# A two-layer block on one core: x loaded behind the weights, the prologue sorted by group, and the third group's projections moved into the recurrence

## What is computed

```python
q, k, v = silu(x @ Wq), silu(x @ Wk), silu(x @ Wv)          # x is layer-normed first
log_f = log_sigmoid(x @ Wf1 @ Wf2)
gamma = -sigmoid(x @ Wg)
k = l2norm(k);  a = k * gamma[..., None]                    # 16 heads of 8
def step(S, inp):                                           # over the 1024 tokens
    S1 = S + a[:, None] * (k @ S)[None]
    S2 = exp(gf)[:, None] * S1
    S3 = S2 + a[:, None] * (k @ S2)[None] + k[:, None] * v[None]
    return S3, q @ S3
out = layernorm(o * sigmoid(x @ Wo1 @ Wo2)) * ln_w @ Wout
x = x + out                                                 # only the last third of the o rows is used
x = x + shared_ffn(layernorm(x)) + top1_of_16_experts(layernorm(x))
```

## Time and profile before

| | us |
|---|---|
| median of 3 runs | 670.8 (670.62 to 671.29) |
| the profiled execution | 673.13 |
| its span, first to last instruction | 671.4 |
| busy in the span: PE, DVE, ACT, POOL | 528.3, 492.5, 248.9, 360.0 |
| mean granted TensorE clock, share of full | 0.917 |
| GpSimd / VectorE / TensorE share of the chain that ended last | 12%, 33%, 30% |

### The profile page before, as it was taken

One profiled execution on the slowest core, in us unless ns is written; L12 is line 12 of the kernel. 1 busy time (PEld: TensorE's weight loads), 2 busy tenths in 40 slices (PEclk: granted clock), 3 DMA queues, 4 the chain that ended last, 5 costly groups with the idle time before them and its releaser, 6 DMA issues.

```text
span 671.4 us, 7382 instructions
## 1 busy us (share of the span) xinstructions
PE 528.3 (79%) x1809; PEld 273.7 (41%) x1810; DVE 492.5 (73%) x809; ACT 248.9 (37%) x515; POOL 360.0 (54%) x349
## 2 busy tenths in 40 slices
PE   1768989999999886877387689879999967578930
PEld 1434434444454433322154455525454255345520
DVE  3369999989898998799589999498999775412201
ACT  1825754444445242111122145533545124135520
POOL 4235767666667575654567333366767574700023
PEclk9868999999999998887799799998999977979985
DMA  9601116700000590000611012300100021112224
GB/s 218 138 0 32 32 42 162 217 0 1 0 1 0 141 356 35 1 0 0 170 35 55 17 48 69 110 15 16 31 23 18 0 52 35 43 56 63 63 80 111
DMA packets 46706, 41.79 MB, mean 62 GB/s; under 512 B 4588, under 2 KB 40248, under 8 KB 46168
## 3 DMA queue, kind: packets, MB, share of 16 engines
q1 hardware_dynamic: 43140, 35.61, 18.9%
q0 software_dynamic: 2400, 5.38, 2.7%
q10 hardware_dynamic: 1136, 0.46, 0.3%
...
## 4 chain that ended last, share of the span: by engine, by line
DVE 33%; PE 30%; issue 16%; POOL 12%; DMA 5%; ACT 2%; ACTq 1%; POOLq 0%; DVEq 0%; SPq 0%
DVE grown L1412 9%; PE ps L1874 6%; DVE early L1527 5%; POOL grown L1062 4%; DVE ps L1451 4%; PE ps L1831 4%; PE ps L1891 3%; DVE early L1532 3%; PE ps L1832 2%; PE ps L1931 2%; DVE grown L1439 2%; POOL uv L978 2%; PE ps L1639 2%; DVE grown L1405 2%; POOL early L1009 2%
## 5 line engine op out<-in xcount | busy, mean ns | idle before, releaser
L1062 POOL TENSOR_TENSOR grown<-grown 128x512 f32<-128x512 f32 x64 | 80.8, 1272 | 101.4 <-DVE grown L1439 101.4
L1412 DVE TENSOR_TENSOR grown<-ps,steps 128x1536 f32<-128x1536 f32 x64 | 112.1, 1752 | 1.8
L1831 PE MATMUL ps<-grown,cst 128*128 128x512 f32 x128 | 77.7, 692 | 27.8 <-DVE grown L1412 27.6
L857 ACT ACTIVATE uv<-ps 128x512 f32<-128x512 f32 x64 | 38.1, 597 | 110.5 <-DVE grown L1439 110.5
L1874 PE MATMUL ps<-steps 128*128 x128 | 69.6, 642 | 8.8 <-issue 8.6
L1832 PE MATMUL ps<-grown,cst 128*128 128x512 f32 x128 | 71.4, 641 | 0.0
L978 POOL TENSOR_TENSOR uv<-uv,steps 128x512 f32<-128x512 f32 x64 | 67.7, 1081 | 1.7 <-ACT uv L857 1.6
L1310 DVE TENSOR_TENSOR e_h<-rk,ps 128x256 f32<-128x256 f32 x64 | 25.4, 417 | 53.8 <-ACT rk L870 34.0
L1839 PE MATMUL ps<-uv,cst 128*128 128x512 f32 x128 | 60.4, 594 | 0.4 <-POOL uv L978 0.4
L1117 POOL TENSOR_TENSOR early<-state,qT 128x512 f32 x22 | 37.2, 1690 | 32.4 <-DVE state L1426 32.4
L1088 POOL COPY early<-early 128x32 f32<-128x32 f32 x63 | 27.5, 436 | 43.9 <-DVE early L1532 43.9
...
...
## 6 DMA issues: line engine op xcount, KB each, us to landing
...
```

The lines of the kernel that those rows point to most:

```text
L1062: G.tensor_tensor(decayed[:, h], decayed[:, h], work[:, h, 1], ALU.add).then_inc(s_add[h], 1)
L1412: V.tensor_tensor(grown[:, :, h].rearrange("p e (x w) -> p e x w", w=HD), st, per_col(tile, FF, 3, h, HD), ALU.mult).then_inc(s_prod[h], 1)
L1831: T.matmul(bank[2 * h + 1], c["block"], work[:, h, 1], start=True, stop=True).then_inc(s_usum[h], 1)
```

## The change

- SP loads x in four parts: groups 0 and 1, group 2, then, only after the constants and all weights but Wq have landed, the other 12 tiles of the first 21, and the last 11. The weights have three semaphores: Wk and Wv, the five small ones, Wq.
- The batches of the layer norm are tiles 0 to 4, 5 to 20 and 21 to 31.
- ScalarE gets two one-column activations, which load the Sqrt table before the first variances are there, and the Silu table right behind the first root.
- TensorE begins with the transposes and K of group 0; `low` and `wfo` (the products of the small weights) come between. ScalarE, GpSimd and VectorE have group 0 ahead of group 1 likewise.
- The start copies of the state move ahead of the statistics of the third part of x and wait only for their own two banks; the other banks are waited for where TensorE first writes them. c_keys(0) moves behind the first pass, the statistics of the last 11 tiles behind the second, c_keys(1) into step 1's corrections, p_of(1) into the loop.
- K and V of group 2 move into step 0's `front`, G and F into step 1's.

```diff
+    if i == 0:
+        found += [("K", 2), ("V", 2)]
+    if i == 1:
+        found += [("G", 2), ("F", 2)]
...
-FIRST = [("low", 0, 7), ("wfo", 0, 7), ("xT", 0, 0), ("xT", 1, 1), ("K", 0, 2), ("K", 1, 3), ("V", 0, 4), ("V", 1, 5),
-         ("squares", 0, 6), ("squares", 1, 7), ("G", 0, 0), ("F", 0, 1), ("G", 1, 2), ("F", 1, 3), ("xT", 2, 4),
-         ("rk", 0, 5), ("rk", 1, 6), ("K", 2, 0), ("V", 2, 1), ("c", 0, 7), ("c", 1, 2), ("G", 2, 3), ("F", 2, 4)]
+FIRST = [("xT", 0, 0), ("K", 0, 2), ("low", 0, 7), ("xT", 1, 1), ("V", 0, 4), ("K", 1, 3), ("wfo", 0, 7), ("V", 1, 5),
+         ("squares", 0, 6), ("squares", 1, 7), ("G", 0, 4), ("F", 0, 5), ("G", 1, 1), ("F", 1, 3), ("rk", 0, 6),
+         ("rk", 1, 7), ("xT", 2, 4), ("c", 0, 6), ("c", 1, 5)]
...
+        warm = sb("warm", [P, 2])
...
-        s_cst, s_cst2, s_xf, s_wa = sem("s_const"), sem("s_const_rest"), sem("s_xf"), sem("s_attn_weights")
-        s_x = [sem(f"s_x_part{k}") for k in range(3)]
+        s_cst, s_cst2, s_xf, s_wa = sem("s_const"), sem("s_const_rest"), sem("s_xf"), sem("s_low_weights")
+        s_wkv, s_wq = sem("s_key_value_weights"), sem("s_query_weights")
+        s_x = [sem(f"s_x_part{k}") for k in range(4)]
...
-        LN_BATCH = [5, 25]
+        LN_BATCH = [5, 21]
...
-            split = GROUPS[1][0]
-
...
+            first, third = GROUPS[1][0], GROUPS[2][0]
...
-                sp.dma_start(xr1[b * C:(b + 1) * C, split:, :], x_tokens(b, split, L1)).then_inc(s_x[0], 16)
+                sp.dma_start(xr1[b * C:(b + 1) * C, first:, :], x_tokens(b, first, L1)).then_inc(s_x[0], 16)
...
-                sp.dma_start(xr1[b * C:(b + 1) * C, 0:split, :], x_tokens(b, 0, split)).then_inc(s_x[1], 16)
+                sp.dma_start(xr1[b * C:(b + 1) * C, third:first, :], x_tokens(b, third, first)).then_inc(s_x[1], 16)
+            sp.wait_ge(s_cst, 16)
+            sp.wait_ge(s_wa, 80)
+            sp.wait_ge(s_wkv, 32)
...
-                sp.dma_start(xr2[b * C:(b + 1) * C, :, :], x_tokens(b, L1, NT)).then_inc(s_x[2], 16)
+                sp.dma_start(xr1[b * C:(b + 1) * C, 0:third, :], x_tokens(b, 0, third)).then_inc(s_x[2], 16)
+            for b in range(B):
+                sp.dma_start(xr2[b * C:(b + 1) * C, :, :], x_tokens(b, L1, NT)).then_inc(s_x[3], 16)
...
-            for dst, src in ((wqkv[:, 1], "Wk"), (wlow[:, 0], "Wf1"), (wlow[:, 1], "Wo1"), (wup[:, 0], "Wf2"),
-                             (wup[:, 1], "Wo2"), (wgs[:], "Wg"), (wqkv[:, 2], "Wv"), (wqkv[:, 0], "Wq")):
+            act.dma_start(wqkv[:, 1], a["Wk"]).then_inc(s_wkv, 16)
+            for dst, src in ((wlow[:, 0], "Wf1"), (wlow[:, 1], "Wo1"), (wup[:, 0], "Wf2"), (wup[:, 1], "Wo2"),
+                             (wgs[:], "Wg")):
...
+            act.dma_start(wqkv[:, 2], a["Wv"]).then_inc(s_wkv, 16)
+            act.dma_start(wqkv[:, 0], a["Wq"]).then_inc(s_wq, 16)
...
+            S.activation(warm[:, 0:1], eps[:], ACT.Sqrt)
...
+            S.activation(warm[:, 1:2], eps[:], ACT.Silu)
+            evict("xT", 0, xnT[0][:, 0:wide_of(0)], cols=wide_of(0))
+            evict_slot("K", 0, K, ACT.Silu)
+            k_square(0)
...
+            evict("xT", 1, xnT[1][:, 0:wide_of(1)], cols=wide_of(1))
+            evict_slot("V", 0, VV, ACT.Silu)
+            evict_slot("K", 1, K, ACT.Silu)
+            k_square(1)
...
-            for n in (0, 1):
-                evict("xT", n, xnT[n % 2][:, 0:wide_of(n)], cols=wide_of(n))
-            for n in (0, 1):
-                evict_slot("K", n, K, ACT.Silu)
-                k_square(n)
-            for n in (0, 1):
-                evict_slot("V", n, VV, ACT.Silu)
+            evict_slot("V", 1, VV, ACT.Silu)
...
-            for n in (0, 1):
-                evict_slot("G", n, Y, ACT.Sigmoid)
-                evict_slot("F", n, FF, ACT.Sigmoid)
-                spread_rk(n)
+            evict_slot("G", 0, Y, ACT.Sigmoid)
+            spread_rk(0)
+            evict_slot("F", 0, FF, ACT.Sigmoid)
+            spread_rk(1)
+            evict_slot("G", 1, Y, ACT.Sigmoid)
+            evict_slot("F", 1, FF, ACT.Sigmoid)
...
-            evict_slot("K", 2, K, ACT.Silu)
-            k_square(2)
-            evict_slot("V", 2, VV, ACT.Silu)
-            evict_slot("G", 2, Y, ACT.Sigmoid)
-            evict_slot("F", 2, FF, ACT.Sigmoid)
...
-            pool.wait_ge(s_wa, 128)
+            pool.wait_ge(s_wa, 80)
...
-            for n in (0, 1):
-                gate_keys(n)
-                y_of(n)
-                y_keys(n)
-            for n in (0, 1):
-                p_of(n)
+            gate_keys(0)
+            y_of(0)
+            y_keys(0)
+            gate_keys(1)
+            y_of(1)
+            p_of(0)
+            y_keys(1)
...
-                if i in NEED[2:]:
+                if i in NEED[1:]:
...
+            def begin(h):
+
+                V.tensor_copy(bank[2 * h].rearrange("p (x w) -> p x w", w=HD),
+                              c["diag8"].unsqueeze(1).to_broadcast([P, P // 2, HD])).then_inc(s_state[h], 1)
+
...
-            ln_shift(0)
...
+            ln_shift(0)
...
+            ln_stats(LN_BATCH[0], ORDER.index(GROUPS[3][0]))
+            dve.wait_ge(s_cst, 16)
+            for h in (1, 0):
+                dve.wait_ge(s_taken[2 * h], PORT_FIRST[2 * h])
+                begin(h)
...
-            ln_stats(LN_BATCH[0], LN_BATCH[1])
+            ln_stats(ORDER.index(GROUPS[3][0]), LN_BATCH[1])
...
-            ln_shift(1)
...
+            ln_shift(1)
...
-            c_keys(0)
-            ln_stats(LN_BATCH[1], NT)
-            c_keys(1)
...
-            def begin(h):
-
-                V.tensor_copy(bank[2 * h].rearrange("p (x w) -> p x w", w=HD),
-                              c["diag8"].unsqueeze(1).to_broadcast([P, P // 2, HD])).then_inc(s_state[h], 1)
-
...
-            for b in range(6):
-                dve.wait_ge(s_taken[b], PORT_FIRST[b])
-            for h in (1, 0):
-                begin(h)
-                step(h, 0)
-            front(0)
+            step(1, 0)
+            c_keys(0)
+            step(0, 0)
+            dve.wait_ge(s_x[3], 16 * B)
+            ln_stats(LN_BATCH[1], NT)
...
+                if i == 1:
+                    c_keys(1)
...
+                if kind == "Q":
+                    pe.wait_ge(s_wq, 16)
...
-            pe.wait_ge(s_wa, 128)
+            x_transposes_of(0)
+            pe.wait_ge(s_wkv, 32)
+            project("K", 0)
+            pe.wait_ge(s_wa, 80)
...
+            x_transposes_of(1)
+            project("V", 0)
+            project("K", 1)
...
-            for n in (0, 1):
-                x_transposes_of(n)
-            for kind in ("K", "V"):
-                for n in (0, 1):
-                    project(kind, n)
+            project("V", 1)
...
+            rk_over_heads(0)
+            rk_over_heads(1)
...
-            for n in (0, 1):
-                rk_over_heads(n)
-            project("K", 2)
-            project("V", 2)
-            for n in (0, 1):
-                head_sum(n)
-            project("G", 2)
-            project("F", 2)
+            head_sum(0)
...
+                if i == 0:
+                    pe.wait_ge(s_taken[2 * h + 1], PORT_FIRST[2 * h + 1])
...
+                if i == 0:
+                    pe.wait_ge(s_taken[4 + h], PORT_FIRST[4 + h])
...
+                else:
+                    head_sum(1)
```

## The result

The changed kernel takes **666.89 us** (median of 5 runs, 666.41 to 667.84) where the kernel before takes 670.8 (669.66 to 671.29): a ratio of 0.9947, 95% interval [0.9932, 0.9961]. That is faster, but by 3.9 us and not by 9.4; 661.4 was forecast. The profiled execution took 666.89 with a span of 665.1, 6.3 less than the span before, whose own execution lay 2.3 above its median.

A forecast was written before the change was run, and what follows sets the result against it. Bound by a chain of waits before the loop, opening with the last attention weight's transfer, and a full settled loop: −15.8 at the first pass, +2.7, +1.2, +2.5 in steps 0 to 2, sum −9.4, 661.4 us; range 658 to 667.

The forecast's parts named there:

- Mark A: Start of the loop's first pass: forecast to move from 40.90 to 25.1 us, 15.8 earlier.
- The weights: Prologue: weights taken as landed by 7.5 us, with 0.58 MB of x and 0.42 MB of weights and constants asked for.
- Rival 2: Prologue: weights do not land earlier, their queue taking turns with x; first pass at 31, −3 us, 668; chance 0.12.
- q10's 12.2%: First 16 us: the weights' queue keeps 16 engines busy 1.95 us, so its own packets do not explain landing at 13.3.
- Pace of TensorE: Prologue: slow K, V and eight records of group 1 assumed; at 2.4 GHz, −1.5 and −1.0 us more.
- Step 0: Loop: head sum of group 1 comes last, +2.7 us; with TensorE at 2.4 GHz the statistics come last, step 10.3.
- Step 1: Loop: K, V and square sums of group 2 queue ahead of the step's sums on TensorE, +1.2 us.
- step 2: Loop: a new Sqrt table load delays the last root and VectorE's reciprocal, +2.5 us.
- B: Start of the same loop pass in step 3: forecast to move from 66.45 to 57.0 us.
- What is gained at B should stay: After step 3's pass: same rows in same order, reloads tied to loop steps, so the −9.4 us should last.
- rivals 3 and 4: Clock slower in steps 1 to 3, +11, 682 (0.03); gain taken back later, within 1 us of no change (0.04).
- Rival 1: Third group's work hides better in the loop, TensorE entering at 2.4 GHz: −12 to −13 us, 658; chance 0.13.

The follow-up runs named there:

- the experiment: Changed kernel with GpSimd's two buffer clearings made to wait until group 1 is normalized: 662.46 us, ratio 0.987 to the kernel before.
- x not held: Changed kernel with GpSimd's clearings behind group 1's normalization and SP's three waits ahead of the rest of x removed: 663.93 us, ratio 0.9892.
- three fixes: Changed kernel with clearings behind group 1's normalization, last layer-norm root moved to step 0, four waits added to VectorE's queue: 659.23 us; again, ratio 0.9795.
- the second set: Changed kernel timed again without an edit, beside new runs of the kernel before: 663.89 us, ratio 0.9881.

## Why the prediction was wrong

It said −9.4 and the result is −3.9. By its own steps:

1. **Mark A failed**: 28.97, not 25.1. The step is the sentence in which GpSimd's `wge` "moves ahead with its weight". I counted that copy and not the two clearings behind it, and so put the wait of VectorE at nothing. They moved from 13.6 to 7.7, onto VectorE's first normalization: 3.2 us by the experiment at equal pace, and K of group 1 stood at 15.19 where I had 11.9. From there to A my 13.2 us were 13.8. Without the lock and at the slow pace A was at 25.6 and 25.9 (x not held, three fixes), where I had 25.1.
2. **The weights** landed in time, for another reason than the one I gave: I took the load asked for until 7.5 us, which was right, but would have credited SP's wait; the cut of x's second part does it alone. Rival 2's outcome didn't come (the last weight landed at 8.0). But q10's 12.2%, which I set against it, was no argument: in the kernel before the weights did wait, for what x had asked for ahead of them.
3. **Pace of TensorE.** I took 2.07 and 1.49 for K and V and 2.08 for the eight records and gave −2.5 to the other case. Either happens: 28.97 or 25.48, and it is worth 3.0 of these 3.5, not 2.5. In the first profile K, V and the square sums were all slow, and the last eight records, which I had slow, were fast (1.16).
4. **Step 0** came as the case I named and set aside: TensorE at 2.4 GHz, the statistics last, 9.96 (I gave 10.3). +0.82 where the sum had +2.7.
5. **Step 1** +1.31 (forecast +1.2) and **step 2** +2.19 (+2.5) were right, with the releasers named. Step 1 isn't stable, though: with the same loop it took 9.41 to 10.86 by kernel and execution, and 10.24 in the second profile of the changed kernel. B gained 7.61; with only the clearings later it gained 13.5 (66.45 − 52.97). In the second profile of the changed kernel A was 15.4 earlier and B 10.3, near my 15.8 and 9.4, by luck: the lock that I hadn't cost 3.2, and the faster pace that I had left out gave back 3.0.
6. **"What is gained at B should stay" failed**: 7.61 first became 9.4 at the start of the forward recurrence (the 27th step gave 0.8, the next 0.4, what lies between the loop and the recurrence 0.5) and then 6.3. The forward recurrence took 2.0 more, by what three records fewer on VectorE's queue do to a race. What lies behind it took 1.2 more (148.2 against 147.0), but the second profile of the kernel before has 148.4 there, so this isn't the change's.
7. **The base.** The profile of before lay 2.3 above its median and that of after on its own. A difference of 6.3 between the profiles is one of 3.9 between the medians. In the second set it was 8.5, near the forecast; my range of 658 to 667 held both medians (666.89, 663.89).

The rivals 3 and 4 (slower, no change) didn't come. Rival 1 had the clock of step 0 right and not the time.
